# Two attentions on one core: each head's stack stands twice, in rows 0-63 and 64-127, and the two halves of a score tile come from the two halves of the array's rows

## The reference, cut to what matters

```python
# layer 0
xn = layernorm(x)                                   # x: (4, 1024, 128)
d2 = maximum(q2[..., :, None] + k2[..., None, :] - 2.0 * qk, 1e-12)
attn = softmax(-sqrt(d2));  out = (attn @ v) @ wo.T + bo
x = x + out + mixture(xn)      # a shared expert and one of 7 experts per token
# layer 1
xn = layernorm(x)
att = softmax(q @ k.T * scale, over keys)
out = (att summed over keys, times v of its own row) @ w_out.T + b_out
x = x + out + sqrt(real**2 + imag**2)   # real, imag = xn @ cos(..), xn @ sin(..)
```

## Time and profile before

| | |
|---|---|
| median of 3 runs (range) | 1765.18 us (1764.28 to 1782.97) |
| profiled execution | 1764.49 us, span 1762.8 us |
| mean granted TensorE clock | 0.725 of full speed |
| busy: PE / DVE / ACT | 85% / 76% / 82% |
| chain that ended last | PE 42%, ACT 37%, DVE 13% |
| layer 0 rounds, first to last score step | about 54.9 to 1117 us |
| layer 1 score tiles | about 1196 to 1748 us |

### The profile page before, as it was taken

One profiled execution on the slowest core, in us unless ns is written; L12 is line 12 of the kernel. 1 busy time (PEld: TensorE's weight loads), 2 busy tenths in 40 slices (PEclk: granted clock), 3 DMA queues, 4 the chain that ended last, 5 costly groups with the idle time before them and its releaser, 6 DMA issues.

```text
span 1762.8 us, 21320 instructions
## 1 busy us (share of the span) xinstructions
PE 1495.4 (85%) x7910; PEld 501.7 (28%) x7910; DVE 1342.3 (76%) x2465; ACT 1449.4 (82%) x716; POOL 408.0 (23%) x258
## 2 busy tenths in 40 slices
PE   4669697789988999989899899757988998989897
PEld 2113021123344324424314314422322242232112
DVE  5657573676978878898678768667987996998676
ACT  2476859395999999999979978936987977979996
POOL 2245250020740221122012012233212212130101
PEclk8557585565989979999869859886665656575556
DMA  5404123301213111111001011324123023102001
GB/s 142 138 10 132 53 82 99 91 9 30 83 26 128 37 30 31 39 33 34 24 27 40 25 27 31 73 74 85 27 94 70 23 90 70 28 18 99 23 27 48
DMA packets 100032, 99.18 MB, mean 56 GB/s; under 512 B 40402, under 2 KB 75346, under 8 KB 99922
## 3 DMA queue, kind: packets, MB, share of 16 engines
q1 hardware_dynamic: 95506, 86.72, 17.7%
q0 software_dynamic: 4416, 11.02, 2.4%
HBM read 52.75 MB, written 44.96 MB: 55 GB/s over the span
## 4 chain that ended last, share of the span: by engine, by line
PE 42%; ACT 37%; DVE 13%; issue 4%; SPq 2%; DMA 1%; POOL 1%; ACTq 0%; DVEq 0%; POOLq 0%
ACT scores L589 14%; ACT scores L578 13%; PE pvb L534 12%; PE ring L1058 11%; PE ring L519 11%; ACT exp L1075 7%; DVE exp L1081 5%; DVE scores L553 3%; PE aux L1021 1%; ACT L589 1%; PE ring L337 1%; PE pvb L542 1%; ACT ht L837 1%; DMA at<-att 1%; PE aux L1116 1%
## 5 line engine op out<-in xcount | busy, mean ns | idle before, releaser
L553 DVE TENSOR_SCALAR scores<-ring 128x1024 f32<-128x1024 f32 x512 | 602.1, 1216 | 171.7 <-PE ring L519 171.4
L1075 ACT ACTIVATE exp<-ring 128x1024 f32<-128x1024 f32 x512 | 473.2, 1207 | 107.8 <-PE ring L1058 106.4
L578 ACT ACTIVATE scores<-scores 128x8192 f32<-128x8192 f32 x60 | 419.2, 7025 | 125.2 <-DVE scores L553 125.0
L534 PE MATMUL pvb<-scores,val 128*9 128x256 f32 x4096 | 385.7, 459 | 83.4 <-ACT scores L589 65.4
L1058 PE MATMUL ring<-stk 72*128 72x512 bf16 x1024 | 422.1, 558 | 35.6 <-ACT exp L1075 32.4
L589 ACT ACTIVATE scores<-scores 128x8192 f32<-128x8192 f32 x64 | 445.9, 7019 | 0.2
L1081 DVE SCALAR_TENSOR_TENSOR exp<-exp 128x512 f32<-128x512 f32 x512 | 382.7, 768 | 57.4 <-ACT exp L1075 56.8
L519 PE MATMUL ring<-stk 72*128 72x512 bf16 x1024 | 384.8, 467 | 18.9 <-DMA stk<-sum_rows 13.9
L1058 PEld LDWEIGHTS ring<-stk 72*128 72x128 bf16 x1024 | 78.5, 110 | 365.8 <-ACT exp L1075 285.9
L534 PEld LDWEIGHTS pvb<-scores,val 128*9 128x9 f32 x4096 | 67.7, 91 | 361.7 <-issue 358.3
L519 PEld LDWEIGHTS ring<-stk 72*128 72x128 bf16 x1024 | 68.5, 104 | 287.9 <-issue 223.2
(11 more groups left out here) (225 smaller groups left out, 1162.7 us busy)
## 6 DMA issues: line engine op xcount, KB each, us to landing
stk<-stack SPq DMA_DIRECT2D x128, 192.0 KB, 2.9
stack<-qp SPq DMA_DIRECT2D x8, 768.0 KB, 3.8
stack<-kp SPq DMA_DIRECT2D x8, 768.0 KB, 6.9
xj<-xg SPq DMA_DIRECT2D x12, 384.0 KB, 3.8
yg<-yj POOLq DMA_DIRECT2D x12, 384.0 KB, 3.3
stack<-qp SPq DMA_DIRECT2D x8, 512.0 KB, 4.6
stack<-kp SPq DMA_DIRECT2D x8, 512.0 KB, 5.6
xg<-attg SPq DMA_DIRECT2D x5, 512.0 KB, 5.1
```

What stands on the lines that cost most here:

```text
L534: mm = nc.tensor.matmul(pvb[place % 2][32 * c:32 * c + VW, 0:256], val[place][:, j, :], S[place][:, j * N + c * 256:j * N + (c + 1) * 256] ...
L553: nc.vector.tensor_scalar(S[place][:, j * N:(j + 1) * N], tile, 1e-12, None, ALU.max).then_inc(o.release(("qk", group, place, j)), 1)
L578: nc.scalar.activation(S[place][:], S[place][:], ACT.Sqrt).then_inc(root_done, 1)
L1075: nc.scalar.activation(EX[i // 2][:, i % 2, :], tile, ACT.Exp, scale=SCALE1).then_inc(o.release(("qk1", n, i)), 1)
```

## The change

Each stack is loaded twice, into rows 0 to 53 and again into rows 64 to 117 of a tile that now has 128 rows. The first matmul of a score tile (columns 0 to 511) reads rows 0 to 63, the second (columns 512 to 1023) rows 64 to 127. Number, order and output of the matmuls stay; each contracts 64 rows instead of 72. Semaphore counts follow the doubled loads.

```diff
-KROWS = 72
+SIDES = [slice(0, 64), slice(64, 128)]
-        stk0 = [left(f"stk0_{i}", [KROWS, 2, N], BF16) for i in range(2)]
+        stk0 = [left(f"stk0_{i}", [P, 2, N], BF16) for i in range(2)]
...
         def load_stack0(sp, n, slot, done):
-            sp.dma_start(stk0[slot][0:SUM_ROW], d["stack0"][n * HD:(n + 1) * HD].rearrange("e r s t -> (e r) s t")
-                         ).then_inc(done, 16)
-            sp.dma_start(stk0[slot][SUM_ROW:ROWS], d["sums0"][n]).then_inc(done, 16)
+            for side in SIDES:
+                sp.dma_start(stk0[slot][side.start:side.start + SUM_ROW],
+                             d["stack0"][n * HD:(n + 1) * HD].rearrange("e r s t -> (e r) s t")).then_inc(done, 16)
+                sp.dma_start(stk0[slot][side.start + SUM_ROW:side.start + ROWS], d["sums0"][n]).then_inc(done, 16)
...
         def pe_scores0(pe, o, group, place, j):
...
-                pe.wait_ge(stk_in[slot], 32 * (2 * group + place // 2 + 1))
+                pe.wait_ge(stk_in[slot], 64 * (2 * group + place // 2 + 1))
...
-            for cols in HALVES:
-                mm = nc.tensor.matmul(tile[:, cols], stk0[slot][:, K, j * P:(j + 1) * P], stk0[slot][:, Q, cols],
+            for side, cols in zip(SIDES, HALVES):
+                mm = nc.tensor.matmul(tile[:, cols], stk0[slot][side, K, j * P:(j + 1) * P], stk0[slot][side, Q, cols],
                                       start=True, stop=True)
...
         def scores1(out, place, i):
-            for cols in HALVES:
-                mm = nc.tensor.matmul(out[:, cols], stk1[place][:, Q, i * P:(i + 1) * P], stk1[place][:, K, cols],
+            for side, cols in zip(SIDES, HALVES):
+                mm = nc.tensor.matmul(out[:, cols], stk1[place][side, Q, i * P:(i + 1) * P], stk1[place][side, K, cols],
                                       start=True, stop=True)
```

More of the change, by code:

```diff
@@ L221, in build @@
         qp1, kp1 = right("qp1", [P, 3, N], BF16), right("kp1", [P, 3, N], BF16)
-        stk1 = [right(f"stk1_{i}", [KROWS, 2, N], BF16) for i in range(GROUP)]
+        stk1 = [right(f"stk1_{i}", [P, 2, N], BF16) for i in range(GROUP)]
         room.close()
@@ L1052, in load_stack1 @@
         def load_stack1(sp, n, done):
-            sp.dma_start(stk1[n % GROUP][0:SUM_ROW], d["stack1"][n * HD:(n + 1) * HD].rearrange("e r s t -> (e r) s t")
-                         ).then_inc(done, 16)
+            for side in SIDES:
+                sp.dma_start(stk1[n % GROUP][side.start:side.start + SUM_ROW],
+                             d["stack1"][n * HD:(n + 1) * HD].rearrange("e r s t -> (e r) s t")).then_inc(done, 16)
         def scores1(out, place, i):
-            for cols in HALVES:
-                mm = nc.tensor.matmul(out[:, cols], stk1[place][:, Q, i * P:(i + 1) * P], stk1[place][:, K, cols],
+            for side, cols in zip(SIDES, HALVES):
+                mm = nc.tensor.matmul(out[:, cols], stk1[place][side, Q, i * P:(i + 1) * P], stk1[place][side, K, cols],
                                       start=True, stop=True)
@@ L1063, in pe_scores1 @@
             if i == 0:
-                pe.wait_ge(stk1_in[n % GROUP], 16 * (n // GROUP + 1))
+                pe.wait_ge(stk1_in[n % GROUP], 32 * (n // GROUP + 1))
             tile = o.begin(pe, ("qk1", n, i))
@@ L1175, in general0 @@
                             for cols in HALVES:
-                                mm = nc.tensor.matmul(ring[0][:, cols], stk0[0][:, Q, i * P:(i + 1) * P],
-                                                      stk0[0][:, K, cols], start=True, stop=True)
+                                mm = nc.tensor.matmul(ring[0][:, cols], stk0[0][SIDES[0], Q, i * P:(i + 1) * P],
+                                                      stk0[0][SIDES[0], K, cols], start=True, stop=True)
                             mm.then_inc(g_s, 1)
@@ L1223, in general1 @@
                         if i == 0:
-                            eng.wait_ge(g1_in, 16 * GROUP * (u + 1))
+                            eng.wait_ge(g1_in, 32 * GROUP * (u + 1))
                         if k:
```

## The result

The changed kernel takes 1666.2 us (median of 4 runs, 1661.6 to 1671.6) against 1764.7 us for the kernel before in the same comparison: ratio 0.948, 95% interval [0.944, 0.953]. But it is not the forecast's case. It is the first rival's, the clock rises too, which gave 1669 us and a chance of 0.20; the range was drawn wide enough to hold it.

A forecast was written before the change was run, and what follows sets the result against it. No engine was taken to bound all: PE at the low clock, DVE at the high one, ACT in late rounds. Savings of 37 + 3.5 + 24 + 9 - 3 = 70.5 us from 1764.5 gave 1694 us, range 1660 to 1740.

The forecast's parts named there:

- the forecast's case: Whole kernel: halves of each score pair overlap, clock falls where it did; 1694 us, own range 1675 to 1712, chance 0.47.
- the first rival: Layer 0: the clock rises too, DVE bounds rounds 1 to 4; -54 there, late rounds -32, 1669 us, chance 0.20.
- the price of the pair: Two score matmuls of a tile, side by side: 0.54 us for 0.96 at low clock, 0.32 for 0.53 at high.
- who is next: Layer 0: DVE is the engine behind PE in rounds 1 to 4; late rounds can't go below ACT's 60.1 us.
- the terms of rounds 1 to 4 and of the late rounds: Layer 0: 0.42 us off each low-clock pair; 37 us in rounds 1 to 4, 24 in late rounds.
- The signs of the prediction: Expected profile of the changed kernel; for rounds 1 to 4 about 71, 71, 75 and 69 us, DVE busy above 70%.
- The slow rival: Layer 0: clock falls where it now holds, as the array does less; +50 late, +30 early, 1807 us, chance 0.07.
- What was said against this rival: Late rounds: unchanged value products are half the high-clock work, and wide expert matmuls end every fall; also PE busy at 0.50.
- Round 0: First round of layer 0: DVE busy 44.3 of 51.2 us, at most 6.9 can go; half taken, 3.5 us.
- Layer 1: Shorter pairs bring the first tile behind each of 30 preparation items 0.2 to 0.4 us sooner; 9 us.
- The sign of 95 to 100 us of idle time: Layer 1: ACT's idle time for score tiles was to be 95 to 100 us, its even spacing unchanged.
- Loads: Doubled stack loads: nearly all hidden; first stacks, router's constants in round 3 and three batch starts cost 3 us.

The follow-up runs named there:

- the other trace of the same layer 0: Kernel with the score pair changed in layer 1 alone, layer 0 as in the kernel before; 1761.9 us, ratio 0.993.
- the third chip: Chip where the change (1703.1 us), 128 rows without overlap (1694.3), pair in layer 0 with 128 rows in layer 1 (1688.4) and the change without second load (1690.4) ran.

## Why the prediction was right, and where it failed

The time lies in the stated range, but by the mechanism that the prediction had put at 0.20, not by its own: that the number fits is partly luck.

**Right: the price of the pair.** 0.54 and 0.32 us, as taken. The Trainium skill (TensorE: Matmul & The Clock Gate, Part 3), which has matmuls on different row groups run together, agrees with the trace.

**Right: who is next.** DVE is busy for 48.5 of 68.2 us in round 1 and late rounds end at ACT's 60.1 us, as worked out for the first rival. Of PE's waits for a stack only the first of each layer is left, 15.2 and 3.5 us.

**Failed: the terms of rounds 1 to 4 and of the late rounds.** Both counted pairs at the low clock and took 0.42 us off each, "if the clock falls where it did". It still fell, behind the same kind of wait of PE, but didn't stay low. The stretches went to 2.4 GHz after a few steps, so the value products got shorter too, from 0.98 to 0.55 us a step, and DVE set the pace. 37 us were forecast for the first and 55.6 measured, 24 for the second and 32.2. (By the other trace of the same layer 0 it would be 39 and 41; the clock of the stretches, not the split of the gain, is what shows the failure.) The first rival had this at 54 and 32, with a chance of 0.20. Its reason, the same score columns on more rows in the same time, fits the experiments with 64, 96 and 128 rows, but layer 1 of the change does not fit it. What spoke against it, that long stretches stayed low through full-array transposes, told of 72 rows alone.

The signs of the prediction did not match its own term: 71, 71, 75 and 69 us for rounds 1 to 4 are 286, 46 us less than before, where the term takes off 37.

**The slow rival** had the clock fall in late rounds since the array does less. Its premise was right and its conclusion wrong: in the late rounds PE was busy for less, 353.8 of 443.7 us, 47.9 a round where round 6 had 55.24, and the clock was 0.95 all the same. With 64 rows and no overlap it did stay low, in three late rounds of 80.6, 80.7 and 80.2 us. What was said against this rival was misread in part: the three long stretches of the kernel before ended inside the 32 steps, two steps or less behind the transposes of a place (the rise is at 649.9, 912.2 and 1059.1), and not in the wide expert matmuls, which come later. The rule of the Trainium skill that the prediction named here (TensorE: Matmul & The Clock Gate, Why this matters for your kernels) is that a TensorE kept busy gets the full clock and one with gaps loses it. On gaps the trace agrees, as in the 3.69 us ahead of 631.65. On busy time it doesn't: PE was busy throughout at 0.50.

**Round 0:** 3.5 forecast, 0.5 measured. Without the second load the first root of round 1 comes at 136.9 us and with it at 140.4, so the loads may have taken the gain. But kernels with the same round 0 as before reach this root between 136.6 and 139.4 us, so 3 us can't be told here.

**Layer 1:** 9 forecast, 13.6 measured (11.5 between the two kernels that change one layer each). The mechanism was right, its clock stayed low, and the term was somewhat small: the waits behind items became 0.26 us shorter on average, as taken (0.2 to 0.4), and two fewer. The sign of 95 to 100 us of idle time was just missed, at 93.4. On the third chip layer 1 of the change took 10 us more (547.0), 4.3 of them a wait of ACT marked "remote" that the first trace doesn't have, so the agreement should not be read too closely.

**Loads:** 3 forecast, 12.7 measured on one chip. The prediction counted what was queued behind SP's issues, and those waits sum to 6. What it did not price is the data: 79.5 MB read from device memory where it was 52.8, and a stack landing after 3.3 us where it was 2.9. That these make up the rest is not shown.

**The sum.** 70.5 us were forecast and 102.9 measured between the profiled executions, 32.4 more. The stages gave 18.6 + 8.2 + 4.6 + 1.1 more than forecast (the last between the layers, not priced) and round 0 gave 3 less, which is 29.5; the other 3 are the forecast's deduction for loads, which in the measured stages is inside. If the loads cost here what they cost on the third chip, 12.7 us, they hid a part of what the clock gave, and the two wrong terms partly cancelled.

## What to carry to other kernels

Before a short contraction is split over the array, try to widen it with rows of zeros: here one constant gave the whole gain of the change, with half of its loads. Price a shorter or narrower matmul twice, once at the clock of the trace and once at the clock that it may lead to; the second was the larger term here. A second copy of an operand is not free because its issue is hidden: here it cost 12.7 us where the waits counted beforehand came to 3. And before a gain is split between stages, look at a second trace of the unchanged stage; here the split moved by 17 us.

## What the runs showed of the hardware that was not expected

**Busy isn't enough for the clock, and more rows shorten the time that it stays low.** In layer 1, PE was busy for 493.7 of 551.8 us with 72 rows at clock 0.60, and for 359.3 of 530.6 us with 128 rows at 0.95. Rows that hold only zeros counted. In the late rounds of layer 0 the clock fell behind waits of PE both before and after the change (2.60 us ahead of 1003.25, 3.69 ahead of 631.65), and what differed was the way back: that stretch of the kernel before lasted until 1059, that of the change until 635. What the chip looks at in detail these runs don't show.

```profile
DVE scores L556 <- remote: 31.8, 4, 18.4
```

It falls between 400 and 437 us, in which DVE is busy for 4.90 us and GpSimd for 29.27, while GpSimd places the tokens by indirect DMAs. Why DVE stands still meanwhile on two chips and not on the other stays open; no run here tests it. The kernel before was not traced on these chips, so whether its 53 to 63 us more have the same cause is open too.
